# Layer norm's mean taken off in the scaled input, not in the projection's accumulation, and the scaled input made one step earlier

## The reference

```python
def _layernorm(x, axis=-1, eps=1e-5):
    m = jnp.mean(x, axis=axis, keepdims=True)
    v = jnp.var(x, axis=axis, keepdims=True)
    return (x - m) / jnp.sqrt(v + eps)
...
q = jnp.einsum('bnd,dk->bnk', x, Wq)     # x: (4, 8192, 1024), after _layernorm
k = jnp.einsum('bnd,dk->bnk', x, Wk)
v = jnp.einsum('bnd,dv->bnv', x, Wv)
scores = jnp.einsum('bnk,bmk->bnm', q, k) * scale
...
x = x + _layernorm(_L0_attn_ref(_layernorm(x, axis=-1), ...))
x = x + _layernorm(_L0_ffn_ref(_layernorm(x, axis=-1), ...))
```

## Time and profile before

| | |
|---|---|
| Time, median of 2 runs | 2838.26 us (2817.29 and 2859.23) |
| Profiled execution, its own time | 2814.41 us |
| Its span, core 6, the slowest | 2812.7 us (all cores: 2802.9 to 2812.7) |
| TensorE matmuls, busy | 2312.1 us (82%), 13253 |
| VectorE busy | 1058.0 us (38%), 2187 |
| ScalarE busy | 498.2 us (18%) |
| mean granted TensorE clock | 0.911 on this core |

### The profile page before, as it was taken

The page is one execution under the profiler, slowest core; times in us unless marked ns, Lnnn a source line. Parts: engine busy times, 40 slices in busy tenths (PEclk is TensorE's granted clock), DMA queues, the critical chain, the costliest instruction groups (busy, mean ns, idle before and its releaser), DMA issues.

```text
span 2812.7 us, 37014 instructions; the slowest of 8 cores (2802.9 to 2812.7 us)
## 1 busy us (share of the span) xinstructions
PE 2312.1 (82%) x13253; PEld 1173.7 (42%) x13253; DVE 1058.0 (38%) x2187; ACT 498.2 (18%) x1026; POOL 61.6 (2%) x102
## 2 busy tenths in 40 slices
PE   1899999999999577568687788878888899988873
PEld 0233333333333244234344454545555555555541
DVE  0453553544544343433434423342322222232333
ACT  1010110110110022112122222222222222222211
POOL 0000000000000000000000000000000000000000
PEclk7899999999999798688799899989999999999986
DMA  9752542542541430212234243253536362654600
GB/s 177 154 133 107 147 137 103 147 135 104 150 140 56 133 122 31 66 55 90 75 106 151 72 168 125 100 195 116 201 105 220 125 225 99 216 180 152 223 31 15
DMA packets 75171, 357.58 MB, mean 127 GB/s; under 512 B 8832, under 2 KB 25728, under 8 KB 43248
## 3 DMA queue, kind: packets, MB, share of 16 engines
q1 hardware_dynamic: 50048, 276.84, 27.7%
q0 software_dynamic: 24944, 78.38, 12.2%
HBM read 324.51 MB, written 58.72 MB: 136 GB/s over the span
## 4 chain that ended last, share of the span: by engine, by line
PE 66%; DVE 19%; issue 4%; ACT 3%; DVEq 3%; another core or an unknown queue 2%; ACTq 1%; DMA 1%; POOL 0%; POOLq 0%
PE psBig L255 36%; PE psS L255 27%; DVE s_xhat L478 5%; DVE s_xov L729 3%; DVEq L149 2%; DVE s_sm L711 2%; DVE s_sm L714 2%; DVE s_xovT L743 2%; PE psT L738 2%; DVE s_x1buf L803 1%; ACT s_sm L721 1%; PE psX L255 1%; DVE s_x1buf L983 1%; ACT s_sm L725 1%
## 5 line engine op out<-in xcount | busy, mean ns | idle before, releaser
L255 PE MATMUL psS<-s_qtile,s_ktile 128*128 128x256 bf16 x4352 | 594.1, 282 | 118.3 <-ACT s_ptb L1038 55.3
L255 PE MATMUL psBig<-s_vtile,s_ptb 128*128 128x512 bf16 x2176 | 579.9, 391 | 48.2 <-DVE s_ptb L1043 29.8
L255 PEld LDWEIGHTS psS<-s_qtile,s_ktile 128*128 128x128 bf16 x4352 | 401.8, 100 | 201.1 <-issue 144.9
L1038 ACT ACTIVATE s_ptb<-psS,s_cst 128x256 bf16<-128x256 f32 x544 | 257.6, 473 | 656.0 <-PE psS L255 642.8
L255 PE MATMUL psBig<-s_xhat,s_wk 128*128 128x512 bf16 x1024 | 280.3, 407 | 28.9 <-DVE s_xhat L478 28.6
L255 PEld LDWEIGHTS psBig<-s_vtile,s_ptb 128*128 128x128 bf16 x2176 | 214.7, 100 | 208.4 <-issue 73.6
L255 PE MATMUL psBig<-s_wv,s_xhat 128*128 128x512 bf16 x1024 | 243.2, 380 | 0.0
L729 DVE TENSOR_SCALAR s_xov<-s_astg,s_sm 128x1024 bf16<-128x1024 f32 x64 | 52.0, 813 | 411.5 <-ACT s_sm L725 410.2
L508 DVE CAST s_kstg<-psBig 128x512 bf16<-128x512 f32 x192 | 132.7, 691 | 195.4 <-PE psBig L255 189.9
L738 PE MATMUL psT<-s_identb,s_xov 128*128 128x128 bf16 x512 | 50.4, 258 | 154.8 <-DVE s_xov L729 154.5
L255 PEld LDWEIGHTS psBig<-s_xhat,s_wk 128*128 128x128 bf16 x1024 | 93.4, 101 | 189.0 <-issue 112.8
(11 more groups left out here) (140 smaller groups left out, 1521.1 us busy)
## 6 DMA issues: line engine op xcount, KB each, us to landing
s_ktile<-kscr SPq DMA_DIRECT2D x88, 1024.0 KB, 5.9
s_vtile<-vscr SPq DMA_DIRECT2D x88, 1024.0 KB, 5.1
s_xs<-xkvC SPq DMA_DIRECT2D x16, 2048.0 KB, 12.2
s_xsbf<-xkvC POOLq DMA_DIRECT2D x16, 1024.0 KB, 14.1
s_xs<-xqC SPq DMA_DIRECT2D x8, 2048.0 KB, 13.9
kscr<-s_kstg SPq DMA_DIRECT2D x16, 1024.0 KB, 3.8
vscr<-s_vstg SPq DMA_DIRECT2D x16, 1024.0 KB, 3.8
s_x0g<-xq POOLq DMA_DIRECT2D x16, 1024.0 KB, 6.4
```

The costliest lines, as they stand in the source:

```text
L255: return lambda t: t.matmul(out=o, lhsT=l, rhs=r, start=start, stop=stop)
L1038: P.op("act", lambda e, psSm=psSm, m=m: e.activation(out=pt_ap(m), in_=psSm[:, 0:256], func=AF.Exp, scale=SCALE, bias=cst[:, 1:2]), reads= ...
```

## The change

The mean is no longer taken off by a ninth matmul in each group, but by VectorE, in fp32, before `xhat` is rounded:

- the one-row matmuls in `p0_proj`, the column sums (`plan_cw`, its three calls), `r_mrb` and the bf16 casts into it are gone; `hold_m` is fp32 now, and a q slab copies it to `r_mr`
- `p0_xhat` has a second fp32 matmul, which spreads `r_mr` over `psS0`, and for each chunk two VectorE operations: x·r into `xtmp0` or `xtmp1` (fp32), then minus `psS0` into `xhat`
- `p0_xhat(t+1)` stands before `p0_proj(t)` in the loop, not behind it

```diff
@@ p0_rows
                 if is_q:
-                    rmrb_ = r_mrb[0:1, buf * 512:(buf + 1) * 512]
...
-                    P.op("dve", lambda e, rmrb_=rmrb_: e.tensor_copy(
-                        out=rmrb_, in_=hold_m[0:1, 0:512]),
-                        reads=["hold_m0", "hold_m1"], writes=[f"r_mrb{buf}"])
+                    P.op("dve", lambda e: e.tensor_copy(
+                        out=r_mr[0:1, 0:512], in_=hold_m[0:1, 0:512]),
+                        reads=["hold_m0", "hold_m1"], writes=["r_mr"])
...
-                P.op("dve", lambda e: e.tensor_copy(out=rmrb,
-                                                    in_=r_mr[0:1, 0:512]),
-                     reads=["r_mr"], writes=[f"r_mrb{buf}"])
@@ p0_xhat
                 P.op("pe", MM(psS[1][:, 0:512], onesf[:], rrr, True, True),
                      reads=["onesf", "r_r"], writes=["psS1"])
+                P.op("pe", MM(psS[0][:, 0:512], onesf[:], r_mr[0:1, 0:512],
+                              True, True),
+                     reads=["onesf", "r_mr"], writes=["psS0"])
                 for i in range(NCH):
-                    P.op("dve", lambda e, i=i: e.tensor_mul(
-                        out=xhat[:, buf * NCH * 512 + i * 512:
-                                 buf * NCH * 512 + (i + 1) * 512],
+                    xt = xtmp0 if i % 2 == 0 else xtmp1
+                    xtk = f"xtmp{i % 2}"
+                    P.op("dve", lambda e, i=i, xt=xt: e.tensor_mul(
+                        out=xt[:],
                         in0=xs32[:, xo + i * 512: xo + (i + 1) * 512],
                         in1=psS[1][:, 0:512]),
                         reads=[f"xs{buf}", "psS1"],
+                        writes=[xtk])
+                    P.op("dve", lambda e, i=i, xt=xt: e.tensor_sub(
+                        out=xhat[:, buf * NCH * 512 + i * 512:
+                                 buf * NCH * 512 + (i + 1) * 512],
+                        in0=xt[:],
+                        in1=psS[0][:, 0:512]),
+                        reads=[xtk, "psS0"],
                         writes=[f"xhat{buf}_{i}"])
@@ p0_proj (k and q; v likewise)
-                            xh(i), i == 0, False),
+                            xh(i), i == 0, i == NCH - 1),
                             reads=[wkey, f"xhat{buf}_{i}"], writes=[bank])
-                    P.op("pe", MM(psBig[:, (o % 4) * 512:(o % 4 + 1) * 512],
-                                  crow[0:1, o * 128:(o + 1) * 128], rmrb,
-                                  False, True),
-                         reads=[ckey, f"r_mrb{buf}"], writes=[bank])
@@ the stage
                 p0_rows(slabs[0])
-                plan_cw(wk, cwk, "wk", "cwk")
                 p0_xhat(slabs[0])
-                plan_cw(wv, cwv, "wv", "cwv")
...
                     if t + 2 < nsl:
                         p0_dma_xs(slabs[t + 2])
+                    if t + 1 < nsl:
+                        p0_xhat(slabs[t + 1])
                     p0_proj(slabs[t])
-                    if t == 0:
-                        plan_cw(wq, cwq, "wq", "cwq")
...
-                    if t + 1 < nsl:
-                        p0_xhat(slabs[t + 1])
```

More of the change, by code:

```diff
@@ L343, in _plan @@
             wv = sb0("wv", [128, NCH * D], BF16)
-            cwq = sb0("cwq", [1, D], BF16)
-            cwk = sb0("cwk", [1, D], BF16)
-            cwv = sb0("cwv", [1, D], BF16)
             xs32 = sb0("xs32", [128, 2 * NCH * 512], F32)
@@ L358, in _plan @@
             r_mr = sb0("r_mr", [1, 512], F32)
-            r_mrb = sb0("r_mrb", [1, 1024], BF16)
             hold_r = sb0("hold_r", [1, 512], F32)
[L361 to L374, removed]
+            hold_m = sb0("hold_m", [1, 512], F32)
+            xtmp0 = sb0("xtmp0", [128, 512], F32)
+            xtmp1 = sb0("xtmp1", [128, 512], F32)
             def p0_dma_xs(sl):
@@ L433, in p0_rows @@
                 rrr = r_r[0:1, 0:512]
-                rmrb = r_mrb[0:1, buf * 512:(buf + 1) * 512]
                 P.op("dve", lambda e: e.tensor_scalar_mul(
@@ L490, in p0_proj @@
                                     buf * NCH * 512 + (i + 1) * 512]
-                rmrb = r_mrb[0:1, buf * 512:(buf + 1) * 512]
                 wten = wq if is_q else wk
                 wkey = "wq" if is_q else "wk"
-                crow = cwq if is_q else cwk
-                ckey = "cwq" if is_q else "cwk"
                 for o in range(NCH):
@@ L538, in p0_proj @@
                                 wv[:, i * D + h * 512: i * D + (h + 1) * 512],
-                                i == 0, False),
+                                i == 0, i == NCH - 1),
                                 reads=[f"xhat{buf}_{i}", "wv"],
                                 writes=[bank])
[L542 to L546, removed]
                         P.op("dve", lambda e, s4=s4, h=h, bs=bs:
```

## The result

The changed kernel takes 2876.35 us (median of 11 runs) against 2817.74 (10 runs): ratio 1.0201, 95% interval 1.0183 to 1.0218. It is slower by 2.0%. Forecast were 2848 and a range of 2802 to 2895.

A forecast was written before the change was run, and what follows sets the result against it. TensorE was taken to bound the projection stage. Seven cycles +53.2, last q slab -12.3 and start -7.4 gave +33.5 us on the profiled 2814.4, so 2848 us (+1.2%), range 2802 to 2895.

The forecast's parts named there:

- E: The moment when the last matmul group of a slab gives up TensorE; times within a slab are counted from it.
- fifth group: Projection's fifth matmul group, waiting for a psBig copy behind sixteen VectorE operations: 21.8 us into slabs with k/v next, else 16.2.
- clock loss behind the fifth group: In the projection, time lost to a lower clock after waits: 1.75 us per slab, for 23 slabs.
- a cycle: Three projection slabs (q, k/v, k/v), seven times in the stage: 113.6 us against 106.0, +7.6 each.
- end of slab 1, against before: Start of the projection stage: slab 1 would end at 164.1 against 171.5, a gain of 7.4 us.
- The two stops: TensorE waits per slab: for the row chain (3.3 us), and before the fifth group (idle 6.1 or 5.8 us).
- the rival built on it: Projection groups: row matmul worth only its stream, each group 0.20 us dearer, +46 over 228 groups, 2894 us; 6%.
- the second broadcast costs 0.94: On TensorE before the projection, the added broadcast of the mean takes 0.94 us, read at 171.50 to 172.44.
- xhat starts at E+8.4: On VectorE with k/v next, xhat's operations start 8.4 us after E, once the row work ends, and end at E+20.9.
- The early load: At the start, the third xs load (2 MB) is issued into the weight loads and costs 5.9 us, 0 if room.
- the clock that stays low: Rival for the projection: stops keep the clock low, 5.3 us each, +82, 2930 us; 12%.
- The stalls don't come: Rival for the projection: neither wait appears, cycle 81.9 us, -188 in all, 2626 us; 5%.

The follow-up runs named there:

- work spread: Changed kernel with the next slab's broadcasts and sixteen xhat VectorE operations spread between the projection's groups and copies: ratio 0.948, lowest runs 2665.5 and 2666.1 us.
- the first experiment: Changed kernel with p0_xhat(t+1) put back behind p0_proj(t), all else kept: ratio 1.0282, 2896 us.

## Why the prediction was right, and where it was off

Right in direction and mechanism, and within its range (+1.2% forecast, +2.0% measured, 2876 in 2802 to 2895). Its middle is 28 us low: 34 us of loss were forecast and 59 came. The measured ratio stands at the 2% line itself (1.0183 to 1.0218), to whose near side the forecast gave 77% and to whose far side 18%. By its own steps, on core 3:

| Step | Forecast | Measured |
|---|---|---|
| a group without the row matmul | 1.73 | 1.74 |
| wait for the row chain | 3.3, 15 times | 3.31, 15 times (49.8 in all) |
| first broadcast, slab with k/v next | E+6.9 | E+6.92 |
| the two broadcasts | 0.94 each | 1.84 each in all seven q slabs; 0.93 and some 1.5 in k/v with k/v next; 0.94 each in k/v with q next |
| fifth group, q slab / k/v with k/v next / k/v with q next | 21.8 / 21.8 / 16.2 | 23.3 / 22.0 / 16.2 on average (23.25 / 21.98 / 16.4 in the first cycle) |
| clock loss behind the fifth group, same order | 1.75 each | 1.6 / 1.6 / 2.8 on average |
| a cycle | 113.6 | 116.0 |
| end of slab 1, against before | -7.4 | +0.7 (cores 0, 1, 2: -4.3, -7.2, -3.3) |
| last q slab, against before | -12.3 | -12.2 (13.98 against 26.20) |
| the rest of the kernel | 0 | +8 (core 0: -2) |

**Confirmed.** The two stops come where they were put. Taking away the second alone (copies on ScalarE) gives 129 us back; taking away both (work spread) gives some 210. The 81 between them are what the first is worth once the second is gone; no run takes away the first alone, so how the two share the 210 is not shown beyond that. The removal of the row matmuls gives 115 us when nothing else moves: 0.42 for each of the 320 is 134, and most of the rest came back as waits. So the rule of the Trainium skill on lone small matmuls (TensorE: Matmul & The Clock Gate, section "Why this matters for your kernels"), taken as the whole price, does not hold in this pattern; the rival built on it needed groups of 1.93 and the trace has 1.74.

**The step that was mis-sized** is "the second broadcast costs 0.94", and with it "xhat starts at E+8.4". I had read the broadcast from a place at full clock and kept that price for both, though I allowed for a lower clock in the four groups behind them. In the q slabs, and in slab 0, the clock is at half already behind the first stop of 3.31 us, and both broadcasts take 1.84. VectorE's chain in the q slab shows the consequence:

```profile
175.65 0.28 DVE L445 COPY s_hold_m<-s_r_mr 1x256 f32<-1x256 f32 x1
176.69 0.69 DVE L463 TENSOR_TENSOR s_xtmp<-s_xs,psS 128x512 f32<-128x512 f32 x1 [0.77 <-PE psS L255]
178.39 0.69 DVE L469 TENSOR_TENSOR s_xhat<-s_xtmp,psS 128x512 bf16<-128x512 f32 x1 [1.01 <-PE psS L255]
```

The row copy ends at 175.93, at E+8.36, within 0.1 us of the forecast, so it isn't VectorE's row work that sets xhat's start, as I had it. The multiplication waits 0.77 for the first broadcast and starts at E+9.12, 0.72 after the forecast E+8.4; the subtraction waits 1.01 more for the second. That makes 1.73, and 1.45 of it shows at the fifth group (23.25 against 21.8). Over a cycle the fifth groups come 1.7 us later than forecast (61.5 against 59.8 for the three), 12 us in seven. The bf16 broadcast took 24 us off the time, but that is more than this term: the pass is cheaper than the 0.94 of the sum at either clock, and the clock fell in other places. "Lower clock in the first four groups costs nothing" was true of the groups and false of the broadcasts ahead of them, which nothing hides.

The clock loss behind the second stop was 0.25 low on average (1.6 + 1.6 + 2.8 against 5.25 a cycle), 5 us over seven cycles. So seven cycles came out 17 us longer than forecast (116.0 against 113.6). Of the rest of the 28, 3 us are the distance of the timed runs of before (2817.7) from the profiled one from which I counted (2814.4). What is left lies in the start (next) and in the rest of the kernel, and differs from core to core.

**The start.** The early load was costed about right: GpSimd issued slab 1's xsbf at 69.34 on core 3 (60.87 there before), and 5.7 to 8.5 later than before on cores 0 to 3, where I took 5.9; it landed at 79.5 (forecast 79.0). On core 3 the broadcasts behind it ran at half clock as well (1.84 each). Slab 1 ends at 163.6 to 167.6 on these cores, where I had 164.1; but I set that against the 171.5 of core 6 alone, which was the late one: on cores 0 to 3 slab 1 ended at 166.8 to 170.7 before. So the gain lies between 7.2 us and nothing, where I took 7.4. No run holds the third load back, so its own price is not shown apart.

**What the prediction did not have.** That the mean's broadcast shares psS0 with the sums of squares. It cost nothing in the changed kernel, so no number was wrong, but it is the one thing that the new place of xhat avoids, and I missed it again in the first experiment, where it made 45 us. It is also what is left of waiting in the spread kernel (29.6 us).

Of the rivals, the clock that stays low had its sign right: half clock rose from 10.6 to 34.8 us per cycle. What it cost behind the fifth groups is 6.0 us a cycle, 1.6 to 2.8 per stop; the rest lies ahead of them, in the stops, the broadcasts and groups 1 to 4, and of that only the slower broadcasts add to the path. Its price of 5.3 per stop was not reached. The Trainium skill (TensorE: Matmul & The Clock Gate, section "A second HAM failure mode: psum-queue depth-cycling") describes the like: bursts over PSUM banks with short pauses between them, and a clock that goes down and up again at a cost. This trace agrees, with a clock of 0.86 in the stage against 0.96, though its stops, 1.5 to 5.6 us, are few and long. "The stalls don't come" was priced at 2626; with the stops removed by hand the kernel takes 2666. Its cycle is 89.1 where 81.9 was counted, and nearly all of the difference is in the k/v slab behind a q slab: 39.8 us in the cycle shown (161.19 to 200.99) where full clock and no wait give 33.1. There the sums of squares wait 3.86 us for the subtraction and then run at half clock (3.57 against 1.89).

## What to carry to other kernels

Before a piece of work is moved ahead of another in a queue that is taken in order, count what each of its instructions waits for and what is queued behind it, on every engine that it touches: here the same instructions took 2876 us in one block ahead of the projection and 2666 us spread between its groups. Price an instruction at the clock of the place to which it goes, not at that of the place where it was read: what comes right behind a new stop can run at half clock, here in some slabs and not in others. And when an operand moves to a bank or buffer that something else uses, look for who writes it next.

## What the runs showed of the hardware

- An fp32 matmul of one row over 512 columns takes 0.94 us at full clock and 1.84 at half clock, two instructions each; the bf16 one in its place 0.56 at half clock (171.03 to 171.59) and 0.31 at full (314.61 to 314.92).
- A one-row matmul between groups of eight costs 0.41 (2.15 less 1.74), about twice the 0.22 of one of the eight (1.74/8).
- The same stop of 3.31 us left the clock at half (1.2 GHz) right behind it in all seven q slabs of the changed kernel (0.50 from 174.5 to 178.1), and at full in all seven k/v slabs with k/v next (the first broadcast took 0.93, 206.22 to 207.15), where it fell during the second broadcast (0.61 from 207.2 to 208.6). Behind stops of 1.49 us it fell too, later: 0.80 from 247.2 to 255.8.
